# Attention scores as three float32r products of split queries and keys, with a new order of all engines' work, in a transformer block with adaptive layer norm

## The reference

```python
def attn(x, Wq, Wkv, Wo, bo):                     # HEADS = 16, DIM_HEAD = 64
    q = (x @ Wq).reshape(B, N, H, Dh).transpose(0, 2, 1, 3)
    k, v = the two halves of x @ Wkv, in the same shape
    s = jnp.einsum('bhid,bhjd->bhij', q * Dh ** (-0.5), k)
    gm = jnp.max(s, axis=-1, keepdims=True)
    p = jnp.where(causal_mask, 0.0, jnp.exp(s - gm))
    num = jnp.einsum('bhij,bhjd->bhid', p, v)
    out = num / (jnp.sum(p, axis=-1, keepdims=True) + 1e-8)
    return out.transpose(0, 2, 1, 3).reshape(B, N, H * Dh) @ Wo + bo

def ffn(x, w_gate, w_up, w_down):                 # 128 -> 352 -> 128
    # fp4_linear: both factors are rounded to FP4 with a scale for each block of 16
    h = silu(fp4_linear(x, w_gate)) * fp4_linear(x, w_up)
    return fp4_linear(h, w_down)

sa, ca, ga, sb, cb, gb = six modulation rows of each batch, from its condition
x = x + ga * attn(layernorm(x) * (1 + ca) + sa, ...)
x = x + gb * ffn(layernorm(x) * (1 + cb) + sb, ...)
```

## Time and profile before

| what | value |
|---|---|
| median of 3 runs | 1324.75 us (1322.56 to 1326.55) |
| the profiled execution's own time | 1323.2 us |
| its span, first to last instruction | 1321.3 us |
| mean granted TensorE clock | 0.988 of full speed |
| busy: PE, PEld | 1270.0 us (96%), 1033.1 us (78%) |
| busy: DVE, ACT, POOL | 1089.7 us (82%), 837.1 us (63%), 841.2 us (64%) |

### The profile page before, as it was taken

How to read it: one execution, slowest core, us unless ns; L and a number is a source line. 1 busy time by engine, 2 the same in 40 slices (tenths; PEclk the granted TensorE clock), 3 DMA queues, 4 the chain that set the end, 5 groups by cost and what they waited for, 6 DMA issues and landing times.

```text
span 1321.3 us, 34181 instructions
## 1 busy us (share of the span) xinstructions
PE 1270.0 (96%) x10194; PEld 1033.1 (78%) x10194; DVE 1089.7 (82%) x2565; ACT 837.1 (63%) x2885; POOL 841.2 (64%) x1582
## 2 busy tenths in 40 slices
PE   4999999999999999999999999999999999999984
PEld 3678888788888788888788888888888878888863
DVE  5678888888888888888888888888888888888775
ACT  3666657667667666666766666766666766666640
POOL 1656666766666766666666666676666676666664
PEclk9999999999999999999999999999999999999995
DMA  3000000000000000000000000000000000000000
GB/s 103 18 19 18 12 22 18 22 22 16 12 20 18 22 22 16 20 12 20 20 22 20 17 10 22 18 22 22 16 11 21 18 22 22 16 22 6 19 19 10
DMA packets 38056, 26.53 MB, mean 20 GB/s; under 512 B 2800, under 2 KB 33392, under 8 KB 38032
## 3 DMA queue, kind: packets, MB, share of 16 engines
q1 hardware_dynamic: 38032, 26.23, 7.0%
HBM read 21.94 MB, written 4.28 MB: 20 GB/s over the span
## 4 chain that ended last, share of the span: by engine, by line
PE 92%; DVE 4%; ACT 2%; issue 1%; DMA 1%; POOL 1%; SPq 0%; DVEq 0%; POOLq 0%; ACTq 0%
PE ps_m L827 27%; PE ps_s L922 18%; PE ps_m L806 16%; PE ps_o L949 14%; PE ps_m L873 9%; PE ps_s L931 5%; PE ps_m L897 4%; ACT probs L563 1%; DMA wkv<-L_attn_Wkv 1%; DVE neg_max L736 1%; DVE probs_t L662 0%; DVE qy L62 0%; ACT qk L531 0%; DVE amax L54 0%; DVE qm L66 0%
## 5 line engine op out<-in xcount | busy, mean ns | idle before, releaser
L563 ACT ACTIVATE probs<-ps_s,neg_max 128x128 f32<-128x128 f32 (+1 forms) x1024 | 424.4, 429 | 396.0 <-PE ps_s L931 396.0
L437 POOL TENSOR_SCALAR probs<-probs,r_den 128x256 f32<-128x256 f32 (+1 forms) x768 | 347.6, 468 | 0.0
L736 DVE TENSOR_REDUCE neg_max<-ps_s 128x4 f32<-128x1024 f32 x256 | 303.9, 1218 | 2.5 <-PE ps_s L922 2.3
L922 PE MATMUL ps_s<-qk 64*128 64x256 f32 x2048 | 259.1, 392 | 0.8 <-ACT qk L531 0.8
L662 DVE COPY probs_t<-ps_m 128x512 f32<-128x512 f32 x256 | 176.4, 689 | 80.2 <-PE ps_m L806 76.2
L806 PE MATMUL ps_m<-ident,probs 128*128 128x128 f32 x1536 | 230.9, 273 | 2.4 <-POOL probs L437 1.0
L435 POOL TENSOR_TENSOR probs<-probs,r_den 128x128 f32<-128x128 f32 x256 | 102.1, 399 | 202.5 <-DVE r_den L745 183.8
L922 PEld LDWEIGHTS ps_s<-qk 64*128 64x128 f32 x2048 | 185.3, 187 | 48.3 <-issue 12.3
L563 ACT ACTIVATION_READ_ACCUMULATOR probs<-ps_s,neg_max 128x1 f32 x1024 | 217.7, 213 | 0.0
L73 POOL TENSOR_TENSOR qy<-qy,qm 128x352 f32<-128x352 f32 (+1 forms) x96 | 82.9, 864 | 181.7 <-DVE qm L66 179.4
L949 PE MATMUL ps_o<-probs_t,v 128*64 128x256 f32 (+1 forms) x2048 | 194.7, 332 | 1.5 <-ACT o_t L555 1.5
(11 more groups left out here) (107 smaller groups left out, 1794.2 us busy)
## 6 DMA issues: line engine op xcount, KB each, us to landing
mod_a<-mod_rows SPq DMA_DIRECT2D x32, 256.0 KB, 3.3
x_in<-L_attn_x SPq DMA_DIRECT2D x32, 128.0 KB, 2.1
x_res<-L_attn_x SPq DMA_DIRECT2D x32, 128.0 KB, 2.1
out<-y_out SPq DMA_DIRECT2D x32, 128.0 KB, 1.8
mod_b<-mod_rows SPq DMA_DIRECT2D x32, 64.0 KB, 2.9
wkv<-L_attn_Wkv SPq DMA_DIRECT2D x2, 512.0 KB, 6.9
wq<-L_attn_Wq SPq DMA_DIRECT2D x1, 512.0 KB, 4.1
wo<-L_attn_Wo SPq DMA_DIRECT2D x1, 512.0 KB, 8.2
```

Of the source, the lines that this page charges most:

```text
L437: ins = nc.gpsimd.tensor_scalar(cols, cols, r_den[:, u % 4, s:s + 1], 1.0, ALU.mult, ALU.mult)
L563: ins = nc.scalar.activation(probs[:, u % 4, h, t * P:(1 + 2 * t) * P], ps_s[:, 2 * (u % 2) + h, t * N:t * N + (1 + t) * P], ACT.Exp, bias ...
L736: nc.vector.tensor_reduce(neg_max[:, u % 4, :], ps_s[:, 2 * (u % 2):2 * (u % 2) + 2, :].rearrange("p b (t j) -> p (b t) j", t=2), AX.X, AL ...
L922: mm = nc.tensor.matmul(ps_s[:, 2 * (u % 2) + h, t * N:(t + 1) * N], qk[rows, u % 4, 0, t * P:(t + 1) * P], qk[rows, u % 4, 1, :], start=( ...
```

## The change

The queries and keys of a unit are no longer kept as one float32 tile `qk` but as two float32r tiles `qk_r[0]` (high) and `qk_r[1]` (low). ACT's copy out of the bank writes the high part; DVE then subtracts it from the bank's content and writes the low part, and only then are the unit's scores released and the bank free. The scores are three float32r products for each half of the rows and each head, again with the two heads in the two halves of the array. Of the twelve `t` copies of a batch ACT now does eight and DVE four (before: four and eight); one of the four copies of `ps_o` goes from ACT to DVE. The order of `SHARED`, and the order of the work on every engine within the blocks, is new.

```diff
-        qk = sb("qk", [P, 4, 2, N])
+        qk_r = [sb(f"qk_r{n}", [P, 4, 2, N], F32R) for n in range(2)]
...
         SHARED = (
-            ("t0", "qk0", "t1", ("v", 0, 0), ("xqt", 2, 0), "qk1", "t2", ("gate", 2, 0), ("v", 0, 1)),
...
+            (("xqt", 2, 0), "qk0", "qk1", ("gate", 2, 0), ("v", 0, 0), "t0", ("up", 2, 0), ("gate", 2, 1), "t1", "t2"),
...
-        T_ON_ACT = (2,)
...
                         elif kind == "qk":
                             act.wait_ge(qk_full, UNITS * b + k + 1)
-                            nc.scalar.copy(qk[:, k % 4, :, :], ps_m[bank][:, :].rearrange("p (n j) -> p n j", n=2)
-                                           ).then_inc(qk_ready, 1)
+                            nc.scalar.copy(qk_r[0][:, k % 4, :, :], ps_m[bank][:, :].rearrange("p (n j) -> p n j", n=2)
+                                           ).then_inc(qk_high, 1)
...
+                    elif kind == "qk":
+                        dve.wait_ge(qk_high, UNITS * b + k + 1)
+                        nc.vector.tensor_tensor(qk_r[1][:, k % 4, :, :], ps_m[bank][:, :].rearrange("p (n j) -> p n j", n=2),
+                                                qk_r[0][:, k % 4, :, :], ALU.subtract).then_inc(qk_ready, 1)
...
                     for t in range(2):
-                        for h in range(2):
-                            rows = slice(h * DH, (h + 1) * DH)
-                            mm = nc.tensor.matmul(ps_s[:, 2 * (u % 2) + h, t * N:(t + 1) * N],
-                                                  qk[rows, u % 4, 0, t * P:(t + 1) * P], qk[rows, u % 4, 1, :],
-                                                  start=(t == 0), stop=True, skip_group_check=True)
+                        for n, (l, r) in enumerate(((0, 1), (1, 0), (0, 0))):
+                            for h in range(2):
+                                rows = slice(h * DH, (h + 1) * DH)
+                                mm = nc.tensor.matmul(ps_s[:, 2 * (u % 2) + h, t * N:(t + 1) * N],
+                                                      qk_r[l][rows, u % 4, 0, t * P:(t + 1) * P], qk_r[r][rows, u % 4, 1, :],
+                                                      start=(t == 0 and n == 0), stop=(n == 2), skip_group_check=True)
                     mm.then_inc(s_full, 1)
...
```

More of the change, by code:

```diff
@@ L567, in exponentials @@
                         ins.then_inc(exp_done, 1)
-                    if has.attn:
-                        exponentials(2 * j, 0)
-                        exponentials(2 * j, 1)
-                    first = 5 if j == 2 else 4
-                    for n in range(first):
-                        shared_reads(n)
-                    if has.attn:
-                        exponentials(2 * j + 1, 0)
-                    for n in range(first, 6):
-                        shared_reads(n)
-                    if j == 1 and has.prev:
-                        out_copy()
@@ L734, in maxima @@
                 def maxima(u):
+                    if not has.attn:
+                        return
                     dve.wait_ge(s_full, UNITS * i + u + 1)
@@ L745, in denominators, with out_copy @@
                     nc.vector.reciprocal(r_den[:, u % 4, :], den_eps[:, u % 4, :]).then_inc(rden_ready, 1)
-                for j in range(PAIRS):
-                    if has.unit(2 * j - 1):
-                        denominators(2 * j - 1)
-                    if has.attn:
-                        maxima(2 * j)
-                    if j == 3 and has.next:
+                def out_copy():
+                    if has.unit(2 * (j - 2)):
+                        at = 2 * ((j - 2) % PAIRS)
+                        dve.wait_ge(o_full, PAIRS * i + j - 1)
+                        nc.vector.tensor_copy(o_t[:, at:at + 2, :], ps_o[:, :].rearrange("p (u j) -> p u j", u=2)).then_inc(ot_ready, 1)
@@ L760, in body, with input_normalized, attended_stats @@
+                def input_normalized():
+                    if has.next:
+                        dve.wait_ge(ln1_pool, 2 * (i + 2))
+                        normalized([xn[:, t, :] for t in range(2)], x_in, mv1, rstd1, xn_ready)
+                def attended_stats():
+                    if has.prev:
                         dve.wait_ge(x1_steps, X1_STEPS * (i - 1) + 2)
                         layer_norm_stats(x1, stats2, mv2, x1_steps, X1_STEPS * (i - 1) + 2)
-                    shared_reads(j, 2)
@@ L774, in body, with attended_normalized @@
-                    if j == 2 and has.prev2:
-                        hidden_scales(i - 2, 1)
-                    if j == 2 and has.prev:
+                def attended_normalized():
+                    if has.prev:
                         dve.wait_ge(ln2_pool, 2 * i)
                         normalized([xn2[:, t * P:t * P + P] for t in range(2)], x1, mv2, rstd2, xn2_ready)
-                    if j == 2 and has.prev2:
-                        hidden_magic(i - 2, 1)
-                    if j == 1 and has.next:
-                        dve.wait_ge(ln1_pool, 2 * (i + 2))
-                        normalized([xn[:, t, :] for t in range(2)], x_in, mv1, rstd1, xn_ready)
```

294 lines of the change are left out of this document (232 added, 62 removed), and 6 rows, old and new, of the table SHARED.

## The result

The changed kernel takes 1330.13 us (median of 6 runs, 1329.88 to 1331.99) where the kernel before took 1323.98 us in the same comparison (6 runs): a ratio of 1.0049, 95% interval 1.0037 to 1.0061. It is slower, by some 6 us, where 1302 us and "faster" were forecast. Its profiled execution has a span of 1330.0 us (1321.3 before).

A forecast was written before the change was run, and what follows sets the result against it. PE's list of products was taken as the bound: 39.24 - 1.28 (scores) + 0.6 (waits) = 38.56 us a batch, 0.68 less, times 31 = 21 us, so 1323.2 becomes 1302 us; eight-in-ten range 1272 to 1345.

The forecast's parts named there:

- What bounds the kernel before: Steady part: PE's own list of products sets the pace, busy 39.09 of 39.24 us a batch, with one 0.4 us wait.
- The scores group: Scores on PE: 24 float32r products, heads paired, take 1.61 us instead of 1.93, saving 1.28 us a batch.
- rival 2: Scores on PE: float32r products do not pair or wait for loads, group 3.05 us, 1462 us in all; chance 0.06.
- that milder form of the rival: Scores on PE: at 81 ns a product, 24 products cost at least 1.94 us, leaving no gain; no separate chance.
- The order's own effect on PE's list: Changes of kind between PE's products under the new order: taken as zero, within 0.4 us a batch.
- The low part and DVE's load: Subtraction on DVE: 0.69 us, eight a batch; DVE then needs 36.9 to 37.9 us a batch.
- Rival 1: DVE becomes the bound through its work and waits: batch 40 us, 1347 us, slower; chance 0.19.
- a sign that I had set: Forecast is wrong if DVE's idle time stays above 3 us a batch while PE idles.
- The waits that come: New PE waits on DVE and ACT in the steady part: 0.6 us a batch counted, full walk 1.2.
- the places that I named: Expected PE waits: end of block 0 (up to 0.4 us), head of block 2 (0.2 to 0.3), block 3 (0.3).
- I leave ramp and tail as they are: Both ends of the span: no change counted, the last two batches' feed-forward chain being the same work in another order.
- Fourth rival: Waits of 1.2 to 1.3 us a batch eat the gain: 1320 to 1327 us; chance 0.08.

The follow-up runs named there:

- e1: The changed kernel with its new order but the float32 scores of before and no subtraction on DVE: 1309.3 us, ratio 0.9877 against the kernel before.
- e4: The changed kernel with four moves: a low part ahead of hidden scales, modulation rows earlier, POOL's weight rounding later, hidden rounding ahead of down in the last turns: 1302.9 us.
- e13: e4 with DVE's copy of ps_o in block 2 moved to ACT, behind ACT's copy of qk0: 1305.0 us.
- e16: e4 with DVE's copy of ps_o moved to ACT at the head of block 2, ahead of the first exponentials: 1304.1 us.
- e3: The changed kernel with one swap in DVE's block 1, the low part of qk1 ahead of the scales of hidden half 1: 1314.7 us.
- e8: The changed kernel with only the first move of e4, modulation rows earlier on DVE and feed-forward weight scales behind block 0 of batch 0: 1326.4 us.

## Why the prediction was wrong

- **What bounds the kernel before: not contradicted.** That PE's list sets the pace there rests on its one wait of 0.4 us; no run takes work off the other engines alone, and e1 shows that such a list can hide 0.13 us a batch.
- **The scores group: right.** 1.63 us for the forecast 1.61, the heads pair (rival 2 out). The Trainium skill (TensorE: Matmul & The Clock Gate, Back-to-back issue gap) gives a sustained spacing of about 81 ns a product at 128 columns; that it is for unpaired products was my reading of it. By the rows 1.63 us for 24 products is 68 ns each, so that milder form of the rival is out too. Over all four groups of a batch the split saves 1.08 us (e4 against e1), not 1.28, since some groups wait for exponentials or low parts.
- **The order's own effect on PE's list: mis-sized.** "I take zero for that and keep +-0.4 a batch." It was -0.82 (e1, with the moved copies), and the price of a change that I had in mind explains 0.17 of it. This error was in my favour: with it the list is 38.39 - 1.08 = 37.3 us, not 37.96, taking e1's distances for its list.
- **The low part and DVE's load: right in size, wrong in meaning.** 0.69 us, 256 of them. DVE is busy for 35.0 us a batch. The forecast's 36.9 stands once for the busy time, from which the normalization's 1.07 was still to come off (35.8), and once for busy time and gaps together with it off. Rival 1, DVE at 40 us, did not happen: e13 and e16 take DVE's time away and gain nothing. But a sign that I had set came true: DVE is idle for 3.9 us a batch while PE idles 0.83. The engines wait for each other, and neither is full. ACT's 27.80 us are what was forecast.
- **The waits that come: this is the step that failed in the steady part.** "I count 0.6 us a batch rather than the full 1.2." The batch is 38.90 with a list of 37.3: 1.6 us of waits and of groups stretched by them. The batch came out within 0.4 us of the forecast's 38.56 only because this error and the one before it have opposite signs, and that is luck. The largest wait, 0.45 us a batch by e3, is at none of the places that I named; of those only block 3 shows one, 0.2 us (its second `qk` group takes 0.97 us, 0.79 in e1). I had walked the order with durations of the kernel before, and one of them, 0.18 us, is 0.92 here, beside a rounding of POOL that it did not meet before. I had counted what the order wins by such a meeting ended (`xn`, 991 to 347 ns), and not looked for one begun.
- **"I leave ramp and tail as they are": this is the step that made it slower.** They cost 10.9 and 7.0 us; e4 and e8 show the places and e4 gets 13.6 of the 17.9 back. Without them the changed kernel would stand at 1330.1 - 17.9 = 1312 us (a sum, not a run), on the forecast's side. In ramp and tail there is no other work to cover a wait, so an order made for the steady part has to be walked there by itself. The order of instructions showed both: set-up behind the first low parts, a rounding behind a read.
- **Fourth rival:** waits that eat the gain, 1320 to 1327, comes nearest in time, but not in kind: the waits did not eat the steady part's gain, the ends did, and those no rival priced.

## What to carry to other kernels

Price the first and last turn of a pipeline by their own walk: a place in an engine's list that costs nothing in the steady part can hold a whole chain there. Before adding an engine between PE and the release of its bank, compare what PE saves with how long the bank is held, not with the engine's spare time: here 0.27 us saved in each scores group stood against 0.69 us of hold in each of eight banks, and the two cancelled. A large edit that changes both the arithmetic and the order needs each run alone; here the order, with its moved copies, was worth 1.9% once its ends were mended, and the arithmetic nothing. And an empty list of waits does not show that an engine never waits: look whether a start follows another engine's end by the same few hundredths of a microsecond in every batch.

## What the runs showed of the hardware

- Float32r products 64 rows deep pair as float32 ones do: 24 of 256 columns in 1.63 us, the two of a pair starting 0.003 us apart.
- A VectorE instruction on 4 or 22 elements a partition took 2.52 and 0.92 us beside POOL instructions of 2.56 and 0.94 us, and 0.17 and 0.18 us otherwise.
- A group of six float32r products of 256 columns takes 0.80 us behind another kind and 0.72 behind its like; one mask product takes 0.11 us among masks and 0.04 between two float32r groups, so that by these rows a mask moved there costs 0.01 us net.
